# Two cross-attention stages rearranged: PSUM banks dealt out anew in the narrow one, VectorE's order and the query copies in the late one

## The chip, the cores and the metric

The kernel runs on one core of a Trainium2 chip. A core has five engines that run side by side and meet only at semaphores: TensorE (PE in the profile; PEld is its weight load), VectorE (DVE), ScalarE (ACT), GpSimd (POOL) and SyncE (SP), which issues the DMAs here. Matrix products land in PSUM, which has eight banks of 2 KiB in each of its 128 partitions; the other tensors lie in SBUF. The metric is device time in microseconds for one execution.

## The reference, cut to what matters

A two-layer decoder works on `x` of 128 sequences of 64 tokens with 128 channels, and every sub-layer is a residual on a layer norm. Six blocks follow each other: a wide self-attention, a cross-attention with narrow heads, a feed-forward block, two narrow self-attentions, and a wide cross-attention with a last tanh product. The change touches the second and the last.

```python
# narrow cross-attention: 16 heads of 8 channels, 64 keys, a mask
q = (layernorm(x) @ Wq.T + bq); k = (ctx @ Wk.T + bk); v = (ctx @ Wv.T + bv)
attn = softmax(q @ k.T / sqrt(8) + mask)
x = x + (attn @ v) @ Wo.T + bo
...
# late cross-attention: 16 heads of 64 channels, and the last product behind it
q = layernorm(x) @ Wq + bq; k = ctx @ Wk + bk; v = ctx @ Wv + bv
x = x + (softmax(q @ k.T / sqrt(64)) @ v) @ Wo + bo
x = x + tanh(layernorm(x) @ W0 @ W1 @ W2 + bias)
```

## The kernel before

The 8192 tokens are cut into 64 tiles of 128 tokens (two sequences), and `x` stays in SBUF as `w_x`. Each block of the model is a stage, and a stage is a software pipeline written out by hand. For each engine `skewed` takes a list of pieces with a lag: in step u the engine runs, in the order of the list, each piece for tile u minus its lag. Every engine works through its list in order, so a piece that waits on a semaphore holds up all that stands behind it in the list. The first 12 steps and the last ones are written out; the steps between them, 52 in both stages, are a loop whose body has four steps.

In the **narrow cross-attention** (tensors `ca_...`, norm `can_...`) a tile goes through: `measure` (VectorE, mean and variance), `rsqrt` (GpSimd), `offset` (VectorE, minus mean times rstd), `apply` (ScalarE, the normalised tile), `turn` and `turned` (transpose, copy out), `project` (queries, keys, values into one bank), `queries_keys` and `values` (ScalarE copies them out), `blocks` (GpSimd spreads the keys), `scores` (PE), `softmax` (VectorE adds the mask and takes the maximum), `shift` (GpSimd subtracts it), `exponent` (ScalarE), `turn_probs` (eight transposes into the two banks `pp0` and `pp1`), `probsT` (two copies out), `attend` (PE: numerator and denominator), `normalise` (VectorE: a reciprocal and a product), `output` (PE), `residual` (VectorE). Four banks, `ca_ss`, hold the scores in their lower halves. Numerator and denominator lie in the upper half of the first of these banks:

```python
num, den = ss[:, 0, 256:384], ss[:, 0, 384:512]
...
after(pe, o_done, t, 4)                                        # scores waits for normalise
...
pe.wait_ge(biased, min(t + 4, NT) * 2 if isinstance(t, int) else (t + 4) * 2)   # attend waits for softmax
```

So `scores` waits until `normalise` has emptied that half, and `attend` waits until `softmax` has read the other half of the same bank.

In the **late cross-attention** (tensors `xa_...`, norms `xan_...` and `lan_...`) the scores of a tile come from eight chunks of queries, of which ScalarE copies all out of PSUM (L909). VectorE's list has 11 pieces, among them `keys` (L947, two copies with the bias), `sums` (L972 and L975: row sums and their inverse), which releases GpSimd's `normalise` (L1015, one product over 128x1024), and `apply_last` (L496 with `lan_xn`), for which PE's `turn_last` (L794) waits. Behind `turn_last` PE's list has `turn` (L786), and the next step begins with `scores` (L851).

Of the kernel before, what the change touches and what calls it, by code (L numbers as in the profile page):

```python
# [710 lines left out]
def wide_cross_attention(k):  # L711
# [6 lines left out]
    with ExitStack() as ctx:  # L718
# [32 lines left out]
        with nc.Block() as block:  # L751
# [27 lines left out]
            def _(pe):  # L779
# [102 lines left out]
            def _(act):  # L882
# [52 lines left out]
            def _(dve):  # L935
# [61 lines left out]
                def finish(t, four):  # L997
# [5 lines left out]
                skewed(dve, NT, [(3, turn_blocks), (5, residual), (7, finish), (2, softmax), (0, measure), (5, measure_last), (1, keys), (2, sums),  # L1003
                                 (0, apply), (5, apply_last), (4, copy_x)], 4)
# [18 lines left out]
def narrow_cross_attention(k):  # L1023
# [7 lines left out]
    with ExitStack() as ctx:  # L1031
# [16 lines left out]
        off = sb("off", [P, 2])  # L1048
# [13 lines left out]
        y_psum, xb_done, x_done, off_done = sem("y_psum"), sem("x_plus_bias"), sem("x"), sem("offset")  # L1062

        with nc.Block() as block:
# [18 lines left out]
            def _(pe):  # L1083
                def turn(t, four):
# [4 lines left out]
                    after(pe, x_done, t, 7)  # L1089
# [13 lines left out]
                def scores(t, four):  # L1103
# [4 lines left out]
                    after(pe, o_done, t, 4)  # L1108
# [7 lines left out]
                def attend(t, four):  # L1116
# [4 lines left out]
                    pe.wait_ge(biased, min(t + 4, NT) * 2 if isinstance(t, int) else (t + 4) * 2)  # L1121
# [13 lines left out]
                def turn_probs(t, four):  # L1135
                    after(pe, exp_done, t)
                    for b in range(2):
                        after(pe, p_done, t, 1, per=2)
# [776 lines left out]
```

## Time and profile before

| | us |
|---|---|
| median of 3 runs (2395.14 to 2398.44) | 2395.47 |
| the profiled execution, its own time | 2399.14 |
| span of that execution in the trace | 2397.3 |
| narrow cross-attention, first statistics to last residual | 545.4 to 904.9 |
| late cross-attention, first statistics to the end | 1690.6 to 2397.3 |

The profile follows one execution. Its own time is 1.8 us more than the span of its instructions and 3.7 us above the median. A row of the timeline gives the start of a group of like instructions, its length, engine, line, operation, names and count; a bracket at its end is idle time of the engine before it and what ended it.

### The profile page before, as it was taken

The page shows a single profiled execution, that of the slowest core. Times are in us where ns is not written, and L with a number is a line of the kernel's source. Part 1 is how long each engine was busy: PE and PEld are TensorE (multiplying, and loading weights), DVE is VectorE, ACT ScalarE, POOL GpSimd, SP SyncE. Part 2 cuts the span into 40 slices and gives each one's busy share as a digit, 9 for nine tenths or more (in the row PEclk, how much of TensorE's full clock was granted, in tenths as well). Part 3 has the DMA queues.
Part 4 walks back from the last instruction along what each step waited for, and adds up shares of the span by engine and source line. Part 5 has one row for each costly group of instructions (what it writes and reads, how often), then busy time and mean ns, then how long its engine had stood idle before and what let it go on. Part 6 is the DMA issues. An engine that isn't in the chain of part 4 may idle for free. (4 is left out here: it accounts for less than half of the span.)

```text
span 2397.3 us, 89507 instructions
## 1 busy us (share of the span) xinstructions
PE 2110.9 (88%) x32271; PEld 1771.4 (74%) x32271; DVE 1924.7 (80%) x5225; ACT 1668.8 (70%) x4485; POOL 1200.5 (50%) x1151
## 2 busy tenths in 40 slices
PE   7999999997777771537999979999799999999997
PEld 7888888885555550235888858888688888888886
DVE  3888888877999986996777667776498999999995
ACT  1676666666777775646888858888476776777674
POOL 0333333326777764107999869999132333333332
PEclk9999999998999995857999989999899999999998
DMA  5000000001111100001000000000133333333333
GB/s 125 3 0 0 0 0 0 0 1 32 31 30 30 30 25 1 1 0 37 1 0 0 0 2 1 0 0 0 52 110 105 115 117 111 115 109 118 113 112 91
DMA packets 112239, 96.98 MB, mean 40 GB/s; under 512 B 24259, under 2 KB 103430, under 8 KB 112134
## 3 DMA queue, kind: packets, MB, share of 16 engines
q1 hardware_dynamic: 108722, 94.39, 12.8%
q10 hardware_dynamic: 3412, 1.19, 0.2%
q8 instruction: 66, 1.08, 0.2%
q14 instruction: 39, 0.32, 0.0%
HBM read 53.59 MB, written 41.94 MB: 40 GB/s over the span
## 5 line engine op out<-in xcount | busy, mean ns | idle before, releaser
L706 POOL TENSOR_TENSOR sa_sc<-sa_sc,sa_rs 128x1024 f32<-128x1024 f32 x64 | 121.8, 1904 | 311.1 <-DVE sa_rs L682 311.1
L1870 POOL TENSOR_TENSOR lo_qk_r<-lo_qk_ms,w_neg_half 128x20 f32<-128x20 f32 x64 | 226.9, 3546 | 22.3 <-DVE lo_qk_ms L1792 22.3
L1870 POOL TENSOR_TENSOR gl_qk_r<-gl_qk_ms,w_neg_half 128x20 f32<-128x20 f32 x64 | 226.3, 3536 | 14.3 <-DVE gl_qk_ms L1792 14.0
L486 POOL TENSOR_TENSOR xan_ve<-xan_mv,w_eps_ln 128x1 f32<-128x1 f32 x64 | 12.1, 189 | 352.8 <-DVE xan_mv L480 352.8
L917 ACT ACTIVATE xa_vx<-xa_oo 64x512 f32<-64x512 f32 x256 | 151.3, 591 | 43.1 <-PE xa_oo L817 38.3
L1015 POOL TENSOR_TENSOR xa_sc<-xa_sc,xa_rs 128x1024 f32<-128x1024 f32 x64 | 122.2, 1909 | 107.3 <-DVE xa_rs L975 107.3
L930 ACT ACTIVATE xa_oT<-xa_oo 128x512 f32<-128x512 f32 x128 | 69.5, 595 | 131.4 <-PE xa_oo L864 131.4
L651 ACT ACTIVATE sa_oT<-sa_oo 128x512 f32<-128x512 f32 x128 | 69.5, 595 | 117.6 <-PE sa_oo L594 117.6
L827 PEld LDWEIGHTS xa_qs<-xan_xT,late_x_wq 128*128 128x128 f32 x1024 | 124.4, 192 | 30.6 <-issue 30.6
L909 ACT ACTIVATE xa_qT<-xa_qs,late_x_bq 128x128 f32<-128x128 f32 x512 | 138.9, 383 | 1.6
L558 PE MATMUL sa_qs<-san_xT,w_a_wq 128*128 128x128 f32 x1024 | 134.0, 285 | 5.4 <-DVE sa_sc L668 5.0
L838 PE MATMUL xa_pp<-xa_cT,late_x_wk 128*128 128x128 f32 x1024 | 131.2, 283 | 0.2 <-DMA xa_cT<-ctxT_kept 0.2
L875 PE MATMUL xa_yy<-late_x_wo,xa_oT 128*128 128x128 f32 x1024 | 128.6, 280 | 1.8 <-ACT xa_oT L930 1.8
L558 PEld LDWEIGHTS sa_qs<-san_xT,w_a_wq 128*128 128x128 f32 x1024 | 121.9, 195 | 10.1 <-DVE sa_sc L668 7.4
L1617 PE MATMUL lo_ss<-lo_qT,lo_kz 128*128 128x256 f32 x512 | 127.9, 393 | 1.4 <-ACT lo_kz L1678 0.9
L1617 PE MATMUL gl_ss<-gl_qT,gl_kz 128*128 128x256 f32 x512 | 127.7, 393 | 1.4 <-ACT gl_kz L1678 0.9
L603 PE MATMUL sa_yy<-w_a_wo,sa_oT 128*128 128x128 f32 x1024 | 126.6, 277 | 1.2 <-ACT sa_oT L651 1.2
L1256 POOL TENSOR_TENSOR ca_sc<-ca_sc,ca_mx 128x1024 f32<-128x1024 f32 x64 | 121.7, 1902 | 11.1 <-DVE ca_mx L1226 8.2
L838 PEld LDWEIGHTS xa_pp<-xa_cT,late_x_wk 128*128 128x128 f32 x1024 | 125.1, 200 | 0.8 <-DMA xa_cT<-ctxT_kept 0.5
L827 PE MATMUL xa_qs<-xan_xT,late_x_wq 128*128 128x128 f32 x1024 | 124.6, 275 | 0.0
L875 PEld LDWEIGHTS xa_yy<-late_x_wo,xa_oT 128*128 128x128 f32 x1024 | 122.7, 196 | 2.5 <-ACT xa_oT L930 2.5
L603 PEld LDWEIGHTS sa_yy<-w_a_wo,sa_oT 128*128 128x128 f32 x1024 | 121.0, 194 | 1.7 <-ACT sa_oT L651 1.7
(323 smaller groups left out, 6714.0 us busy)
## 6 DMA issues: line engine op xcount, KB each, us to landing
blocks<-xa_tb SPq DMA_DIRECT2D x64, 512.0 KB, 2.7
xa_pt<-blocks SPq DMA_DIRECT2D x256, 128.0 KB, 2.9
w_x<-in_x_dram SPq DMA_DIRECT2D x8, 512.0 KB, 7.5
ca_cx<-in_ctx_dram SPq DMA_DIRECT2D x64, 64.0 KB, 1.8
ctxT_kept<-ca_xcT SPq DMA_DIRECT2D x64, 64.0 KB, 1.6
xa_cT<-ctxT_kept SPq DMA_DIRECT2D x64, 64.0 KB, 1.8
out_dram<-xa_out SPq DMA_DIRECT2D x64, 64.0 KB, 1.6
ca_mask<-in_mask_BxSxS_ff_dram SPq DMA_DIRECT2D x64, 32.0 KB, 1.7
```

The source lines that it names most:

```text
L558: last = pe.matmul(qs[b][:, c * P:(c + 1) * P], k["a_wq"][:, ch * P:(ch + 1) * P], norm["xT"][:, s, :], start=True, stop=True)
L603: last = pe.matmul(yy[:, 0:D], oT[:, s, n % 2, n // 2, :], k["a_wo"][:, n, :], start=(n == 0), stop=(n == 7))
L706: pool.tensor_tensor(v, v, bcast(rs[:, s, :], 2, S), ALU.mult).then_inc(prob_done, 1)
L827: final = pe.matmul(qs[b][:, c * P:(c + 1) * P], k["x_wq"][:, ch * P:(ch + 1) * P], norm["xT"][:, s, :], start=True, stop=True)
L838: final = pe.matmul(pp[b][:, c * P:(c + 1) * P], k["x_wk"][:, ch * P:(ch + 1) * P], cT[:, s, :], start=True, stop=True)
L875: final = pe.matmul(yy[:, 0:D], oT[:, s, n % 2, n // 2, :], k["x_wo"][:, n, :], start=(n == 0), stop=(n == 7))
L909: act.activation(qT[:, s, ch, :], qs[b][:, c * P:(c + 1) * P], ACT.Identity, bias=k["x_bq"][:, ch:ch + 1]).then_inc(q_done, 1)
L917: act.activation(vx[u * 64:u * 64 + 64, four, b, :, :, :].rearrange("p m e d -> p (m e d)"), oo[u][b * 64:b * 64 + 64, :], ACT.Copy).then_ ...
L1015: pool.tensor_tensor(v, v, bcast(rs[:, s, :], 2, S), ALU.mult).then_inc(prob_done, 1)
L1256: pool.tensor_tensor(sc[:, four, :, :], sc[:, four, :, :], bcast(mx[:, s, :], 2, S), ALU.subtract).then_inc(shifted, 1)
L1617: last = pe.matmul(ss[b][:, g * 256:(g + 1) * 256], kz[:, s, b, 2 * g:2 * g + 2, :].rearrange("p g j -> p (g j)"), qT[:, s, b, :, :].rearr ...
L1870: pool.tensor_tensor(qk_r[:, s, :], qk_ms[:, s, :], k["neg_half"][:, 0:NQK], ALU.pow).then_inc(sg["qk_r"], 1)
```

## The change: what it does

In the narrow cross-attention the two PSUM banks of the turned probabilities become one (`pp`), and numerator and denominator get the freed bank (`nd`). `turn_probs` and `probsT` are split into two rounds of four transposes and one copy each; the second round on PE waits until the copy of the first is done. The waits of `scores` on `normalise` and of `attend` on `softmax` go. `offset` moves from VectorE to GpSimd, as two products on one column. The lists of PE, ScalarE and VectorE are put in another order, and `output` and `residual` come one step earlier. In the late cross-attention chunks 4 to 7 of the queries are copied out by VectorE in one instruction, with a semaphore of its own for which `scores` waits too, and VectorE's list is put in another order.

```diff
@@ wide_cross_attention
                 def scores(t, four):
-                    after(pe, q_done, t, per=8)
+                    after(pe, q_done, t, per=4)
+                    after(pe, q2_done, t)
...
-                    for b in range(2):
-                        act.wait_ge(q_psum, t * 2 + b + 1)
-                        for c in range(4):
-                            ch = 4 * b + c
-                            act.activation(qT[:, s, ch, :], qs[b][:, c * P:(c + 1) * P], ACT.Identity,
-                                           bias=k["x_bq"][:, ch:ch + 1]).then_inc(q_done, 1)
+                    act.wait_ge(q_psum, t * 2 + 1)
+                    for c in range(4):
+                        act.activation(qT[:, s, c, :], qs[0][:, c * P:(c + 1) * P], ACT.Identity,
+                                       bias=k["x_bq"][:, c:c + 1]).then_inc(q_done, 1)
...
+                def queries(t, four):
+                    s = four % 2
+                    after(dve, s_psum, t, 2)
+                    after(dve, q_psum, t, per=2)
+                    dve.tensor_tensor(qT[:, s, 4:8, :], qs[1][:, :].rearrange("p (c i) -> p c i", c=4),
+                                      bcast(k["x_bq"][:, 4:8], 2, P), ALU.add).then_inc(q2_done, 1)
...
-                skewed(dve, NT, [(3, turn_blocks), (5, residual), (7, finish), (2, softmax), (0, measure), (5, measure_last), (1, keys), (2, sums),
-                                 (0, apply), (5, apply_last), (4, copy_x)], 4)
+                skewed(dve, NT, [(5, residual), (7, finish), (3, turn_blocks), (2, softmax), (0, measure), (5, measure_last), (2, sums),
+                                 (1, keys), (1, queries), (0, apply), (5, apply_last), (4, copy_x)], 4)
@@ narrow_cross_attention
-        pp = [ps("pp0"), ps("pp1")]
+        pp, nd = ps("pp"), ps("nd")
...
-        num, den = ss[:, 0, 256:384], ss[:, 0, 384:512]
+        num, den = nd[:, 0:P], nd[:, P:2 * P]
...
-                    after(pe, o_done, t, 4)
...
-                    pe.wait_ge(biased, min(t + 4, NT) * 2 if isinstance(t, int) else (t + 4) * 2)
...
+                        after(pe, exp_done, t)
+                        if b == 0:
+                            after(pe, p_done, t, 1, per=2)
+                        else:
+                            pe.wait_ge(p_done, t * 2 + 1)
...
-                skewed(pe, NT, [(3, scores), (2, project), (1, turn), (6, attend), (5, turn_probs), (7, output)], 4)
+                skewed(pe, NT, [(6, attend), (3, scores), (5, turn_probs(0)), (2, project), (1, turn), (5, turn_probs(1)), (6, output)], 4)
...
-                skewed(act, NT, [(2, queries_keys), (1, turned), (2, values), (4, exponent), (5, probsT), (0, apply)], 4)
+                skewed(act, NT, [(5, probsT(0)), (2, queries_keys), (1, turned), (5, probsT(1)), (2, values), (4, exponent), (0, apply)], 4)
...
-                skewed(dve, NT, [(8, residual), (0, measure), (3, softmax), (6, normalise), (0, offset)], 4)
+                skewed(dve, NT, [(7, residual), (0, measure), (6, normalise), (3, softmax)], 4)
...
+                    pool.tensor_tensor(neg_mean[:, s:s + 1], norm["mv"][:, s, 0:1], neg_one[:, :], ALU.mult).then_inc(nm_done, 1)
                     norm_rsqrt(k, norm, pool, t, s)
+                    after(pool, norm["rstd_done"], t)
+                    pool.tensor_tensor(off[:, s:s + 1], neg_mean[:, s:s + 1], norm["rstd"][:, s:s + 1], ALU.mult).then_inc(off_done, 1)
```

Two places show the new order. The first is one step of PE in the narrow cross-attention. Before, it is `scores` (L1113), `project`, `turn`, `attend` (L1127, L1131, into `ca_ss`), the eight transposes of the probabilities (L1141) and `output` (L1150):

```order
L1113 MATMUL ca_ss<-ca_kz,ca_qT 64x256 x8
L1099 MATMUL ca_m<-ca_xcT,w_c_wq 128x128
L1100 MATMUL ca_m<-ca_xcT,w_c_wk 128x128
L1101 MATMUL ca_m<-w_c_wv,ca_xcT 128x128
L1090 MATMUL ca_m<-w_constant,can_xn 128x128
L1091 MATMUL ca_m<-w_constant,ca_cx 128x128
L1127 MATMUL ca_ss<-ca_pt,ca_vz 32x64 x16
L1131 MATMUL ca_ss<-ca_pt,ca_vo 32x128 x8
L1141 MATMUL ca_pp<-w_constant,ca_sc 128x128 x8
L1150 MATMUL ca_m<-w_c_wo,ca_oT 128x128
```

After the change the same step on PE, with line numbers of the changed kernel (L1118 is `scores`, L1148 a round of `turn_probs`, L1131 and L1135 `attend`, L1157 `output`):

```order
L1131 MATMUL ca_nd<-ca_pt,ca_vz 32x64 x16
L1135 MATMUL ca_nd<-ca_pt,ca_vo 32x128 x8
L1118 MATMUL ca_ss<-ca_kz,ca_qT 64x256 x8
L1148 MATMUL ca_pp<-w_constant,ca_sc 128x128 x4
L1105 MATMUL ca_m<-ca_xcT,w_c_wq 128x128
L1106 MATMUL ca_m<-ca_xcT,w_c_wk 128x128
L1107 MATMUL ca_m<-w_c_wv,ca_xcT 128x128
L1096 MATMUL ca_m<-w_constant,can_xn 128x128
L1097 MATMUL ca_m<-w_constant,ca_cx 128x128
L1148 MATMUL ca_pp<-w_constant,ca_sc 128x128 x4
L1157 MATMUL ca_m<-w_c_wo,ca_oT 128x128
```

`attend` now opens the step, and the transposes stand in two groups with `project` and `turn` between them.

The second place is the later part of a step of VectorE in the late cross-attention. Before, from the statistics of the last norm on:

```order
L480 BN_AGGR lan_mv<-lan_stats 128x2
L947 TENSOR_TENSOR xa_kT<-xa_pp,late_x_bk 128x512 x2
L972 TENSOR_REDUCE xa_sm<-xa_sc 128x16
L975 RECIPROCAL xa_rs<-xa_sm 128x16
L496 TENSOR_SCALAR xan_xn<-w_x,xan_mv,xan_rstd 128x128
L496 TENSOR_SCALAR lan_xn<-w_x,lan_mv,lan_rstd 128x128
L987 TENSOR_TENSOR xa_xb<-w_x,w_x_row 128x128
L967 STREAM_TRANSPOSE xa_tb<-xa_sc 128x1024
L982 TENSOR_TENSOR w_x<-xa_yy,xa_xb 128x128
L1001 TENSOR_TENSOR xa_out<-xa_yy,w_x 128x128
L954 TENSOR_REDUCE xa_mx<-xa_qs 128x8 x2
```

After the change VectorE has there:

```order
L480 BN_AGGR lan_mv<-lan_stats 128x2
L978 TENSOR_REDUCE xa_sm<-xa_sc 128x16
L981 RECIPROCAL xa_rs<-xa_sm 128x16
L953 TENSOR_TENSOR xa_kT<-xa_pp,late_x_bk 128x512 x2
L945 TENSOR_TENSOR xa_qT<-xa_qs,late_x_bq 128x512
L496 TENSOR_SCALAR xan_xn<-w_x,xan_mv,xan_rstd 128x128
L496 TENSOR_SCALAR lan_xn<-w_x,lan_mv,lan_rstd 128x128
L993 TENSOR_TENSOR xa_xb<-w_x,w_x_row 128x128
L988 TENSOR_TENSOR w_x<-xa_yy,xa_xb 128x128
L1007 TENSOR_TENSOR xa_out<-xa_yy,w_x 128x128
L973 STREAM_TRANSPOSE xa_tb<-xa_sc 128x1024
L960 TENSOR_REDUCE xa_mx<-xa_qs 128x8 x2
```

The row sums and their inverse moved ahead of the key copies, the query copy stands between the keys and the two norms, and the block transpose (`xa_tb`) moved behind the residual and the output sum.

## Rows read from the trace of the kernel before

**Rows 1.** The page's chain that ended last: share of the span by line.

```profile
PE xa_pp L838 5%; PE xa_oo L817 4%; PE xa_yy L875 4%; PE xa_qs L827 4%; PE xa_qs L851 3%; PE xa_oo L864 2%; PE xa_misc L801 1%; PE xa_misc L786 1%; PE xa_misc L794 0%; ACT xa_vx L917 0%; ACT xa_qT L909 0%; DMA blocks<-xa_tb 0%; DMA xa_pt<-blocks 0%; PE xa_yy L808 0%; DVE lan_xn L496 0%
```

**Rows 2.** Windows, four tiles each: length; PE, PEld, DVE, ACT, POOL busy; clock; DMA.

```profile
690.42:712.15 21.73, 17.26 (x339) 12.76 (x328) 20.01 (x38) 17.17 (x45) 16.41 (x21) 1.00 0.11 30
2011.45:2053.03 41.58, 41.06 (x740) 35.32 (x741) 38.93 (x73) 29.52 (x72) 13.29 (x20) 1.00 0.35 114
```

**Rows 3.** Timeline, narrow stage, one step of VectorE and GpSimd: start, length in us.

```profile
700.35 0.29 DVE L1234 TENSOR_TENSOR ca_oT<-ca_ss,ca_rden 128x128 f32<-128x128 f32 x1
700.56 0.75 DVE L1212 SCALAR_TENSOR_TENSOR ca_off<-can_mv,can_rstd 128x1 f32<-128x1 f32 x1
701.24 0.28 DVE L1240 TENSOR_TENSOR w_x<-ca_m,ca_xb 128x128 f32 x1
...
696.85 0.19 POOL L486 TENSOR_TENSOR can_ve<-can_mv,w_eps_ln 128x1 f32<-128x1 f32 x1 [0.86 <-DVE can_mv L480]
...
699.40 1.90 POOL L1256 TENSOR_TENSOR ca_sc<-ca_sc,ca_mx 128x1024 f32<-128x1024 f32 x1
```

**Rows 4.** Timeline, narrow stage, the same step of ScalarE and PE.

```profile
697.42 0.37 ACT L1169 ACTIVATE ca_kT<-ca_m,w_c_bk 128x128 f32<-128x128 f32 x1
697.67 0.38 ACT L1171 ACTIVATE ca_qT<-ca_m,w_c_bq 128x128 f32<-128x128 f32 x1
698.06 0.38 ACT L1163 ACTIVATE ca_xcT<-ca_m 128x256 f32<-128x256 f32 x1
699.36 0.94 ACT L1177 ACTIVATE ca_vz<-ca_m 64x64 f32<-64x64 f32 x4 [0.92 <-PE ca_ss L1131]
700.33 1.06 ACT L1183 ACTIVATE ca_sc<-ca_sc 128x1024 f32<-128x1024 f32 x1
701.41 1.09 ACT L1190 ACTIVATE ca_pt<-ca_pp 128x512 f32<-128x512 f32 x2
...
696.18 0.49 PE L1099 MATMUL ca_m<-ca_xcT,w_c_wq 128*128 128x128 f32 x2
...
696.73 0.39 PE L1101 MATMUL ca_m<-w_c_wv,ca_xcT 128*128 128x128 f32 x2
...
699.24 1.09 PE L1141 MATMUL ca_pp<-w_constant,ca_sc 128*128 128x128 f32 x8
...
700.90 0.69 PE L1113 MATMUL ca_ss<-ca_kz,ca_qT 32*64 32x256 f32 x16 [0.35 <-DVE ca_oT L1234]
```

**Rows 5.** Timeline, late stage, end of a step: VectorE, ScalarE, GpSimd, then PE.

```profile
2006.01 1.29 DVE L947 TENSOR_TENSOR xa_kT<-xa_pp,late_x_bk 128x512 f32<-128x512 f32 x2
...
2008.63 0.26 DVE L496 TENSOR_SCALAR xan_xn<-w_x,xan_mv,xan_rstd 128x128 f32 x1
2008.81 1.97 DVE L496 TENSOR_SCALAR lan_xn<-w_x,lan_mv,lan_rstd 128x128 f32 x1
...
2008.92 2.17 ACT L909 ACTIVATE xa_qT<-xa_qs,late_x_bq 128x128 f32<-128x128 f32 x8
...
2008.80 1.90 POOL L1015 TENSOR_TENSOR xa_sc<-xa_sc,xa_rs 128x1024 f32<-128x1024 f32 x1 [1.71 <-DVE xa_rs L975]
...
2008.89 1.95 PE L875 MATMUL xa_yy<-late_x_wo,xa_oT 128*128 128x128 f32 x16
...
2010.83 0.33 PE L794 MATMUL xa_misc<-w_constant,lan_xn 128*128 128x128 f32 x1
2011.14 0.30 PE L786 MATMUL xa_misc<-w_constant,xan_xn 128*128 128x128 f32 x1
2011.45 1.16 PE L851 MATMUL xa_qs<-xa_kT,xa_qT 64*64 64x64 f32 x64
...
2022.17 0.34 PE L851 MATMUL xa_qs<-xa_kT,xa_qT 64*64 64x64 f32 x8 [0.45 <-issue]
```

**Rows 6.** Timeline, second narrow self-attention: a transpose, then scores, on PE.

```profile
1489.22 0.27 PE L1591 MATMUL lo_misc<-w_constant,lo_hn 128*128 128x128 f32 x1
1489.36 0.89 PE L1617 MATMUL lo_ss<-lo_qT,lo_kz 128*128 128x256 f32 x3
```

More of the change, by code:

```diff
@@ L1088, in turn @@
                     after(pe, xT_done, t, 1)
-                    after(pe, x_done, t, 7)
+                    after(pe, x_done, t, 6)
                     pe.transpose(m1[:, 0:P], norm["xn"][:, s, :], ident).then_inc(norm["xT_psum"], 1)
@@ L1133, in attend, with turn_probs, piece @@
                     last.then_inc(a_psum, 1)
[L1135 to L1138, printed above, removed]
+                def turn_probs(b):
+                    def piece(t, four):
+                        after(pe, exp_done, t)
[3 more added lines that the diff above has]
+                            pe.wait_ge(p_done, t * 2 + 1)
                         for n in range(4):
                             h = 8 * b + 2 * n
-                            last = pe.transpose(pp[b][:, n * P:(n + 1) * P],
-                                                sc[:, four, h:h + 2, :].rearrange("p a b -> p (a b)"), ident)
+                            last = pe.transpose(pp[:, n * P:(n + 1) * P], sc[:, four, h:h + 2, :].rearrange("p a b -> p (a b)"), ident)
                         last.then_inc(p_psum, 1)
+                    return piece
                 def output(t, four):
@@ L1183, in exponent, with probsT, piece @@
                     act.activation(sc[:, four, :, :], sc[:, four, :, :], ACT.Exp).then_inc(exp_done, 1)
-                def probsT(t, four):
-                    s = four % 2
-                    after(act, a_psum, t, 2)
-                    for b in range(2):
+                def probsT(b):
+                    def piece(t, four):
+                        s = four % 2
+                        after(act, a_psum, t, 2)
                         act.wait_ge(p_psum, t * 2 + b + 1)
-                        act.activation(pt[:, s, 4 * b:4 * b + 4, :].rearrange("p a b -> p (a b)"), pp[b][:, :], ACT.Copy).then_inc(p_done, 1)
+                        act.activation(pt[:, s, 4 * b:4 * b + 4, :].rearrange("p a b -> p (a b)"), pp[:, :], ACT.Copy).then_inc(p_done, 1)
+                    return piece
                 def apply(t, four):
@@ L1206, in measure @@
                     norm_measure(k, norm, dve, tile_of(X, t), t, four % 2)
-                def offset(t, four):
-                    s = four % 2
-                    after(dve, norm["rstd_done"], t)
-                    after(dve, norm["xn_done"], t, 2)
-                    dve.scalar_tensor_tensor(out=off[:, s:s + 1], in0=norm["mv"][:, s, 0:1], scalar=-1.0, in1=norm["rstd"][:, s:s + 1],
-                                             op0=ALU.mult, op1=ALU.mult).then_inc(off_done, 1)
                 def softmax(t, four):
@@ L1258, in rsqrt @@
                 def rsqrt(t, four):
-                    norm_rsqrt(k, norm, pool, t, four % 2)
+                    s = four % 2
+                    after(pool, norm["mv_done"], t)
+                    pool.tensor_tensor(neg_mean[:, s:s + 1], norm["mv"][:, s, 0:1], neg_one[:, :], ALU.mult).then_inc(nm_done, 1)
+                    norm_rsqrt(k, norm, pool, t, s)
+                    after(pool, norm["rstd_done"], t)
+                    pool.tensor_tensor(off[:, s:s + 1], neg_mean[:, s:s + 1], norm["rstd"][:, s:s + 1], ALU.mult).then_inc(off_done, 1)
                 def blocks(t, four):
```

10 lines of the change are left out of this document (6 added, 4 removed).

## The prediction

> **What bounds the kernel now.** I read first the page's chain of work that ended last. It ends in the late cross-attention, and nearly all its lines there are PE's [rows 1]: the reader is to see that PE sets the end of the last stage. The chain says nothing of the narrow stage, so second I read the windows, one turn of each loop, four tiles [rows 2]. In the narrow stage a tile takes 21.73 / 4 = 5.43 us, and no engine fills that: VectorE is busy 20.01 / 4 = 5.00, PE 4.32, ScalarE 4.29, GpSimd 4.10. In the late stage a tile takes 41.58 / 4 = 10.40, PE is busy 41.06 of 41.58 and VectorE 38.93. Third I read one step of each timeline, to see what the fullest engine does in its time.
>
> Narrow stage [rows 3]: `offset` (L1212) works on one column and yet lasts 0.75 us. It ends at 701.31, and GpSimd's `shift`, begun at 699.40, ends at 701.30. `offset` cannot finish while `shift` runs. The product before it, L1234, keeps to 0.29 in the middle of the same `shift`. VectorE's next instruction starts 701.24 - 700.56 = 0.68 after `offset` did. So the present step is a ring: VectorE's row maximum releases `shift`, `shift` holds `offset`, `offset` holds VectorE's next step.
>
> Late stage [rows 5]: the same hold. `lan_xn` takes 1.97, its twin `xan_xn` just before it 0.26. It ends at 2010.78, with GpSimd's `normalise` (2008.80 + 1.90 = 2010.70) and 1.71 too late. PE's `turn_last` (L794) waits for it and starts 0.05 later, at 2010.83. PE would hardly have been ready sooner, since L875 has just drained (2008.89 + 1.95). But behind that wait the next single transpose (L786) comes 0.31 later and `scores` (L851) another 0.31 later. Eight such transposes in a row take 1.09 [rows 4], so each needs (1.09 - 0.27) / 7, about 0.12, if the last takes 0.27 like the one in [rows 6]; and where PE does not stand at a wait, `scores` follows a transpose after 0.14 [rows 6]. I read the excess as PE's own preparation of the next pieces (several waits each), which it does early when nothing holds it and late when `lan_xn` does. Where the loop turns round it is worse: from L851 at 2011.45 to the next at 2022.17 are 10.72, while the other three steps share 41.58 - 10.72, 10.29 each: 0.43 more, marked as a wait for nothing [rows 5].
>
> **The change, narrow part.** Without `offset`, VectorE's step could be 5.43 - 0.68 = 4.75. GpSimd takes two more products on a column, 0.19 each like L486 [rows 3], and some 0.1 each to hand over: 4.10 + 0.6 = 4.7. PE and ScalarE keep their work, 4.3 each. The removed waits cost nothing any more: `scores` has its banks for itself as soon as the mask is added. What is late next is a ring that the two rounds make. The exponential of one step must end before PE's first round of transposes, and ScalarE begins its next step with the copy of that round. Its length, from [rows 4]:
> PE: four transposes, then `project`: the eight take 1.09, so `project` can start 0.45 after the first, and it lasts from 696.18 to 697.12, 0.94: 1.39. To ScalarE 0.05 (the shortest hand-over seen, [rows 5]). The first copy lies inside that time. Then ScalarE: keys 0.25 (697.42 to 697.67), queries 0.26 and `turned` 0.27 (0.38 each, less the 0.12 by which the key copy and its follower overlap), second copy 0.50 (two took 1.09, pipelined), values 0.97 (699.36 to 700.33), exponential 1.06. Back to PE 0.26, as `scores` starts 0.26 after L1234 ends (700.64 to 700.90) [rows 3, 4].
> Sum: 1.39 + 0.05 + 0.25 + 0.26 + 0.27 + 0.50 + 0.97 + 1.06 + 0.26 = 5.01. With the short hand-over of 0.05 at the end it is 4.80; with no overlap between ScalarE's three copies (0.38 - 0.26 and 0.38 - 0.27 more) and a hand-over 0.05 longer, 5.29. I take 5.0: it is longer than the sums of VectorE and GpSimd, so it sets the step. The second round's transposes wait for the first copy: round one 0.55, hand-over 0.05, copy 0.59, hand-over 0.26 is 1.45, about when PE has done `project` and `turn` anyway, so I put this wait at nothing; uncovered it could cost 0.1, which the upper end holds. Gain: 0.43 a tile. Some 60 of the 64 tiles run at the steady step: 26 us. Bounds: 4.80 gives 38, 5.29 gives 8.
>
> **The change, late part.** Copies of half the queries go from ScalarE (eight in 2.17, so 1.09 less) to VectorE in one instruction of the form of half L947, 1.29 / 2 = 0.65 [rows 5]. Sums and inverse now come before the keys, so `normalise` starts about 1.29 + 0.65 = 1.94 before the norms are due, and lasts 1.90 with 0.08 to hand over. `lan_xn` then waits some 0.05 instead of 1.71. VectorE's tile becomes 9.73 - 1.71 + 0.65 = 8.67 busy [rows 2, 5], well under 10.3. Its queries wait for PE's last query product, and the norms follow within 0.65 + 0.26 + 0.26 = 1.2, while PE still runs L875 for 1.8. So `lan_xn` comes about 0.6 before PE asks for it. The block transpose comes later by residual and output sum, 0.5, and by their wait for PE's last transpose; the `blocks` transfers behind it are needed a step later. I cost that at nothing.
> PE's work is unchanged. What it can gain is the preparation: 0.31 - 0.12 and 0.31 - 0.14 = 0.36 a step, so 10.29 - 0.36 = 9.93; with the loop's 0.43 kept that is a mean of 10.04, with it gone 9.93. I take 9.97: 0.43 under 10.40, times the 52 steps in the loop, 22 us. The wait added to `scores` (for VectorE's half) stands behind `turn`, where one more wait is at most a third of the 0.17 excess there, 0.06 a tile or 3 us if it shows; hidden it is nothing, and I take nothing. In the first steps, before the pipeline is full, the eight copies lie on the path; 1.09 less in three of them is 3 us. Lower end: nothing but these 3. Upper end: 0.47 x 52 + 3 = 27.
>
> A rule of the Trainium skill bears on the hold. Its page "SBUF — State Buffer", section "Who interferes with whom", says that VectorE and GpSimd share one port pair as an exclusive lock, which an instruction with at most one SBUF input outside the two-port modes does not need. By it the key and query copies, which read PSUM and one SBUF operand, run beside `normalise` and the whole 1.71 goes. The trace agrees as far as L1234 (0.29, one input from PSUM) stands against L1212 (0.75, both from SBUF) under one `shift` [rows 3].
>
> **Sum.** 26 + 22 + 3 = 51 us. On the profiled execution, 2399.1 (2397.3 and 1.8 around it), that is 2348; it stood 3.7 above the median of the runs, 2395.5, from which 51 less is **2344**.
>
> **The rivals.**
> *Only the narrow stage gains* (2 in 10). The 0.31s are what those waits cost PE in this loop, wherever it stands, and the local stage has fewer of them. Late part: the 3 us of the start alone. 2395.5 - 29 = 2366.
> *The ring of the two rounds takes nearly all back* (1 in 10). With 5.29 the narrow part is worth 8, the late 25: 2362. It speaks for it that ScalarE's `turned` may wait for `turn`, which now stands behind four transposes.
> *The hold stays, the slower side* (6 in 100). If the copies of keys and queries are held by `normalise` as `lan_xn` was, VectorE has its hold of 1.71 and 0.65 more work. Occupied for 10.29 less the short wait before its row maxima, say 10.1, it comes to 10.75, and as its residual now waits for PE's last transpose I add 0.3: 11.0 a tile, 0.65 x 52 = 34 us lost against 26 won. 2403. It decides from a hold of about 1.2 us on. L1234 speaks against it.
> *The change doesn't act* (4 in 100). The narrow step stays near 5.4, since three engines lie within 0.7 of it and wait for each other, and PE's preparation stays: within 0.2%, which is 5 us and about what a measurement of this kernel tells from no change.
>
> **How the numbers follow.** The forecast has 60 in 100; its own range, from the bounds of the two terms, is 2330 (38 + 27) to 2358. The first two rivals are added up to 2372 (the first with a narrow step of 5.1): 2328 to 2374 leaves out the slower side, the case of no action and some of the edges, under 2 in 10. Faster by over 0.2%: 0.60 + 0.20 + 0.10 = 0.90. Same 0.04, slower 0.06.
>
> **What would show it.** Narrow: a step near 5.0, no one-column instruction on VectorE, GpSimd near 4.7 a tile, and PE's first round standing at ScalarE's exponential. A step of 4.75 with VectorE full would say that the ring is shorter than I made it. Late: `lan_xn` at about 0.26 to 0.3; L786 and `scores` 0.12 to 0.15 behind their forerunners; a loop of four near 40. If `lan_xn` is short and the 0.31s remain, the first rival holds; if `lan_xn` remains near 2, the third. The prediction is most easily wrong in the late part, where 22 us hang on reading two gaps of 0.31 as preparation that a late norm exposes.

## The result, and the profile after

The changed kernel takes 2329.84 us (median of four, 2326.87 to 2330.55), the kernel before 2395.30 in the same comparison: ratio 0.9725, 95% interval 0.9708 to 0.9742, 65 us off. 2344 was forecast, with a range of 2328 to 2374. The profiled execution took 2330.41, its span is 2328.6, 68.7 under that of before. By stage, from the first row statistics to the last residual or the end of the span: the narrow cross-attention fell from 359.8 (545.4 to 905.2, the end of the last residual) to 327.0 us, the late one from 706.7 to 670.2; the rest grew by 0.6. Between row maxima, as the mean over ten turns of the loop (the 13th to the 53rd), a narrow step fell from 5.43 to 4.77 and a late one from 10.40 to 9.94.

The page of the changed kernel: busy time by engine, and the chain that ended last by line.

```profile
PE 2076.8 (89%) x32271; PEld 1753.6 (75%) x32271; DVE 1832.8 (79%) x5225; ACT 1599.1 (69%) x4229; POOL 1218.7 (52%) x1280
...
PE xa_pp L838 5%; PE xa_qs L827 5%; PE xa_yy L876 5%; PE xa_oo L817 5%; PE xa_qs L852 3%; PE xa_oo L865 2%; PE xa_misc L801 1%; PE xa_misc L786 0%; PE xa_yy L808 0%; PE xa_misc L794 0%; DMA blocks<-xa_tb 0%; DMA xa_pt<-blocks 0%; DVE xa_sm L978 0%; DVE xa_tb L973 0%; ACT xa_sc L922 0%
```

`lan_xn` has left the chain [rows 1]; what is left of the late stage is PE's own work. Windows of the changed kernel over four tiles of each stage, columns as in [rows 2]:

```profile
690.44:709.47 19.03, 16.57 (x328) 12.43 (x328) 17.19 (x33) 16.68 (x45) 17.50 (x29) 1.00 0.13 35
1966.94:2006.70 39.76, 39.47 (x743) 34.66 (x741) 35.35 (x76) 25.43 (x56) 13.29 (x20) 1.00 0.38 119
```

In the narrow stage VectorE lost 2.8 us of busy time in four tiles and GpSimd gained 1.1; all four engines now lie between 4.1 and 4.4 a tile, in a step of 4.76. In the late stage PE is busy for 39.47 of 39.76.

Timeline of the changed kernel, some narrow steps, VectorE, ScalarE, then PE [rows 3, 4]:

```profile
698.85 0.29 DVE L1241 TENSOR_TENSOR w_x<-ca_m,ca_xb 128x128 f32 x1 [0.21 <-POOL ca_xb L1275]
...
699.53 0.18 DVE L480 BATCH_NORM_AGGREGATE can_mv<-can_stats 128x2 f32<-128x6 f32 x1 [0.19 <-DVE can_stats L476]
...
684.63 1.06 ACT L1190 ACTIVATE ca_sc<-ca_sc 128x1024 f32<-128x1024 f32 x1
...
689.33 1.06 ACT L1190 ACTIVATE ca_sc<-ca_sc 128x1024 f32<-128x1024 f32 x1
...
691.81 0.37 ACT L1176 ACTIVATE ca_kT<-ca_m,w_c_bk 128x128 f32<-128x128 f32 x1
...
694.03 1.06 ACT L1190 ACTIVATE ca_sc<-ca_sc 128x1024 f32<-128x1024 f32 x1
...
698.96 1.06 ACT L1190 ACTIVATE ca_sc<-ca_sc 128x1024 f32<-128x1024 f32 x1
...
690.44 0.66 PE L1148 MATMUL ca_pp<-w_constant,ca_sc 128*128 128x128 f32 x4
...
695.29 0.66 PE L1148 MATMUL ca_pp<-w_constant,ca_sc 128*128 128x128 f32 x4
...
700.07 0.66 PE L1148 MATMUL ca_pp<-w_constant,ca_sc 128*128 128x128 f32 x4
```

A ring is a closed chain of work and waits; no step can be shorter than it. The ring of the forecast goes from PE's first round at 690.44 over the keys at 691.81 to the end of the exponential at 694.03 + 1.06 = 695.09, which is 4.65, and with a hand-over of 0.05 it is 4.70. It sets three steps of every four: all through the loop the exponentials start 4.70 apart, and PE's first round follows 0.05 after the exponential (690.39 to 690.44). The fourth step, where the loop turns round, takes 4.92 to 4.97, here from 694.03 to 698.96. In it `attend` starts 0.80 after `output` (692.85 to 693.65) where it otherwise starts 0.44 to 0.49 after (688.15 to 688.59), and the first round comes 0.20 after the exponential (695.09 to 695.29). VectorE does not set the step: it is busy for 4.30 of 4.76, and it waits for its own statistics in every step and for GpSimd's `copy_x` in every second one.

Timeline of the changed kernel, end of a late step, VectorE, GpSimd, then PE over a turn of the loop and one step further [rows 5]:

```profile
1963.79 1.22 DVE L953 TENSOR_TENSOR xa_kT<-xa_pp,late_x_bk 128x512 f32<-128x512 f32 x2
...
1965.99 0.34 DVE L496 TENSOR_SCALAR lan_xn<-w_x,lan_mv,lan_rstd 128x128 f32 x1
...
1963.96 1.90 POOL L1021 TENSOR_TENSOR xa_sc<-xa_sc,xa_rs 128x1024 f32<-128x1024 f32 x1 [0.49 <-DVE xa_rs L981]
...
1966.94 0.27 PE L786 MATMUL xa_misc<-w_constant,xan_xn 128*128 128x128 f32 x1
1967.50 1.16 PE L852 MATMUL xa_qs<-xa_kT,xa_qT 64*64 64x64 f32 x64 [0.29 <-issue]
...
1976.92 0.27 PE L808 MATMUL xa_yy<-w_constant,xa_th 128*128 128x128 f32 x1
1977.03 0.27 PE L794 MATMUL xa_misc<-w_constant,lan_xn 128*128 128x128 f32 x1
1977.14 0.27 PE L786 MATMUL xa_misc<-w_constant,xan_xn 128*128 128x128 f32 x1
1977.35 0.87 PE L852 MATMUL xa_qs<-xa_kT,xa_qT 64*64 64x64 f32 x44
```

`lan_xn` takes 0.34 and ends at 1966.33, half a microsecond before PE uses it (1966.83). L794, L786 and scores follow their forerunners after 0.11, 0.11 and 0.21. At the turn of the loop scores comes 0.56 after L786, so some 0.35 of the turn's excess is still there.

### The profile page after: what moved, and what is told of

Its sections match the earlier page's. It is cut to its first block and busy times, and to the rows that moved or that the text cites. A ratio compares the mean times of both kernels' runs of the same rounds, so it can differ in the third digit from the quotient of the medians.

```text
span 2328.6 us, 89415 instructions
## 1 busy us (share of the span) xinstructions
PE 2076.8 (89%) x32271; PEld 1753.6 (75%) x32271; DVE 1832.8 (79%) x5225; ACT 1599.1 (69%) x4229; POOL 1218.7 (52%) x1280
## 5 line engine op out<-in xcount | busy, mean ns | idle before, releaser
L827 PEld LDWEIGHTS xa_qs<-xan_xT,late_x_wq 128*128 128x128 f32 x1024 | 124.4, 192 | 30.6 <-issue 30.6
L827 PE MATMUL xa_qs<-xan_xT,late_x_wq 128*128 128x128 f32 x1024 | 124.6, 275 | 0.0
L817 PE MATMUL xa_oo<-late_x_wv,xa_cT 128*128 128x512 f32 x256 | 121.1, 595 | 0.0
```

Of the source, the lines that this page charges most:

```text
L817: pe.matmul(oo[u][:, :].rearrange("p (m c) -> p m c", m=4), cT[:, s, :], wv[:, :, u, :], start=True, stop=True).then_inc(v_psum, 1)
L827: final = pe.matmul(qs[b][:, c * P:(c + 1) * P], k["x_wq"][:, ch * P:(ch + 1) * P], norm["xT"][:, s, :], start=True, stop=True)
```

## The experiments

Twelve kernels, each against the kernel before on the same chip. Steps are means over ten turns of the loop between row maxima, as above.

| kernel | median us | ratio to before, 95% | narrow step | late step |
|---|---|---|---|---|
| before | 2395.3 | 1 | 5.43 | 10.40 |
| changed | 2329.8 | 0.9708 to 0.9742 | 4.77 | 9.94 |
| narrow_alone | 2357.4 | 0.9817 to 0.9856 | 4.79 | 10.40 |
| late_alone | 2365.8 | 0.9853 to 0.9895 | 5.44 | 9.95 |
| offset_moved_alone | 2391.0 | 0.9965 to 0.9984 | 5.34 | 10.43 |
| apply_before_copies | 2374.2 | 0.9888 to 0.9917 | 5.04 | 10.41 |
| lists_with_old_banks | 2492.7 | 1.0365 to 1.0426 | 7.68 | 9.95 |
| offset_back_on_vectore | 2328.9 | 0.9695 to 0.9729 | 4.77 | 9.95 |
| copy_in_the_ring | 2334.9 | 0.9726 to 0.9761 | 4.93 | 9.95 |
| copy_in_the_gap | 2326.9 | 0.9695 to 0.9732 | 4.77 | 9.94 |
| order_without_split | 2345.0 | 0.9769 to 0.9806 | 4.77 | 10.19 |
| split_without_order | 2592.5 | 1.0803 to 1.0843 | 4.77 | 14.50 |
| late_norm | 2361.3 | 0.9840 to 0.9876 | 4.79 | 10.52 |
| load_behind_norm | 2327.8 | 0.9702 to 0.9745 | 4.77 | 9.99 |

**The two halves.** `narrow_alone` is the kernel before with the change's hunks in `narrow_cross_attention`; `late_alone` has those in `wide_cross_attention`.

> The kernel before with the narrow stage of the change alone. Theory: the two parts touch different stages and the stages do not overlap by more than their ramps, so the narrow stage falls from 359.8 us to about 327, the late stage keeps its 707 and its loop of four its 41.6: about 33 us off, 2362. Rival, that the two parts help or hinder each other (the narrow stage runs beside something of the late one): the gain differs from 33 by more than 5 us.

> The kernel before with the late stage of the change alone. Theory: the narrow stage keeps its 359.8 us, the late one falls from 706.7 to about 670, of which the steady loop gives 23 to 24 and the first steps about 12: about 36 us off, 2359. Rival, that the gain in the first steps comes from the narrow stage's earlier end or other order: the late stage then stays above 677.

The steps fell just as in the changed kernel. In `narrow_alone` 39 us went, 6 more than forecast and so past the rival's bound of 5: the narrow stage took 324.6 us, and the late stage, untouched, was also 8.5 shorter (698.2). In `late_alone` the late stage took 670.6, as forecast, and 31 us went by the medians (37.6 by the profiled spans). By the medians the parts bring 70 us apart and 65 together, which intervals of 4 to 5 us to either side of each do not tell apart; by the profiled spans they bring 79 and 69. What both bring is in the late stage's first steps. From the first to the twelfth row maximum the late stage takes 121.4 us before, 113.5 in `narrow_alone`, 109.1 in `late_alone`, 109.0 with both.

**Is it the held `offset`?** In `offset_moved_alone` the kernel before gets the change's two products on GpSimd in place of VectorE's `offset`, and nothing else; of the edit, VectorE's list is shown.

```diff
-                skewed(dve, NT, [(8, residual), (0, measure), (3, softmax), (6, normalise), (0, offset)], 4)
+                skewed(dve, NT, [(8, residual), (0, measure), (3, softmax), (6, normalise)], 4)
```

> The kernel before with offset alone moved from VectorE to two products on GpSimd; banks and lists of the narrow stage stay. Theory A (the one-column instruction held under the shift is what the narrow step costs): VectorE's step loses 0.68, the step of 5.43 falls to 4.8 to 4.95, 27 to 35 us off. Theory B (the shared bank, with scores waiting for the output and attend for the mask, sets the step as much): the step stays at 5.3 to 5.4, at most 8 us off.

Theory B's number, though the bank is not yet the longest ring here: the step lost 0.1 of the 0.68. Timeline of `offset_moved_alone`, one step, VectorE, ScalarE, then PE:

```profile
700.25 0.96 DVE L1224 RECIPROCAL ca_rden<-ca_ss 128x128 f32<-128x128 f32 x1 [0.28 <-PE ca_ss L1131]
...
700.25 0.94 ACT L1177 ACTIVATE ca_vz<-ca_m 64x64 f32<-64x64 f32 x4 [0.59 <-PE ca_ss L1131]
...
702.30 1.08 ACT L1190 ACTIVATE ca_pt<-ca_pp 128x512 f32<-128x512 f32 x2
703.27 0.49 ACT L1196 ACTIVATE can_xn<-w_x,ca_off,can_rstd 128x128 f32 x1
...
704.10 0.32 PE L1090 MATMUL ca_m<-w_constant,can_xn 128*128 128x128 f32 x1 [0.86 <-ACT can_xn L1196]
```

In a window of four tiles VectorE is busy 17.73 of 21.29 us, so it no longer sets the step; now it waits for PE's `attend`. PE's list puts `attend` behind `turn`, and `turn` waits 0.86 for ScalarE's `apply`. ScalarE has `apply` behind values, exponential and copies, and values waits for the `attend` of the step. That closes a second ring: values starts at 700.25, when `attend` has ended, `turn` starts at 704.10, and then comes the next `attend`. As the step lost no more than 0.1, the ring must have been there before, at nearly the same length.

`apply_before_copies` cuts that ring in `offset_moved_alone` with one more edit.

```diff
-                skewed(act, NT, [(2, queries_keys), (1, turned), (2, values), (4, exponent), (5, probsT), (0, apply)], 4)
+                skewed(act, NT, [(2, queries_keys), (1, turned), (2, values), (4, exponent), (0, apply), (5, probsT)], 4)
```

> offset_moved_alone with one edit: in ScalarE's narrow list apply stands before the two copies of the probabilities, not behind them. Its trace shows a second ring beside VectorE's: attend ends, values 0.97, exponential 1.08, copies 0.97 to 1.05, apply 0.49 with its hand-over, turn 0.34, attend 1.15: 5.3 a step. Theory A (this ring is why the step stayed at 5.34 when offset left VectorE): without the copies in it the ring is 4.3, and VectorE with the shared bank (mask 1.29, hand-over, attend 1.15, reciprocal 0.96, product 0.32, residual, statistics) sets the step, at 5.0 to 5.25: 5 to 20 us faster than offset_moved_alone. Theory B (the shared bank's ring alone sets 5.34): the step stays within 0.04 of 5.34.

Theory A: 5.04, 16.9 us faster than `offset_moved_alone`. What holds now stands on PE, in the timeline of `apply_before_copies`:

```profile
701.32 0.65 PE L1127 MATMUL ca_ss<-ca_pt,ca_vz 128*32 128x64 f32 x32 [0.52 <-DVE ca_sc L1214]
...
704.00 0.69 PE L1113 MATMUL ca_ss<-ca_kz,ca_qT 32*64 32x256 f32 x16 [0.35 <-DVE ca_oT L1227]
```

Both waits belong to the bank that scores shares with numerator and denominator: `attend` waits for the mask to be added, scores for `normalise`.

**Order or bank?** `lists_with_old_banks` is the changed kernel with the old banks and their waits, and each pair of rounds in one piece:

```diff
-        num, den = nd[:, 0:P], nd[:, P:2 * P]
+        num, den = ss[:, 0, 256:384], ss[:, 0, 384:512]
...
+                    after(pe, o_done, t, 3)
...
+                    pe.wait_ge(biased, min(t + 3, NT) * 2 if isinstance(t, int) else (t + 3) * 2)
...
-                skewed(pe, NT, [(6, attend), (3, scores), (5, turn_probs(0)), (2, project), (1, turn), (5, turn_probs(1)), (6, output)], 4)
+                skewed(pe, NT, [(6, attend), (3, scores), (5, turn_probs), (2, project), (1, turn), (6, output)], 4)
...
-                skewed(act, NT, [(5, probsT(0)), (2, queries_keys), (1, turned), (5, probsT(1)), (2, values), (4, exponent), (0, apply)], 4)
+                skewed(act, NT, [(5, probsT), (2, queries_keys), (1, turned), (2, values), (4, exponent), (0, apply)], 4)
```

> The changed kernel with the narrow stage's banks of before: numerator and denominator back in the scores' first bank with the waits that this needs, the probabilities in two banks, turned and copied in one piece; the lists of the engines, offset and residual as changed. Theory A (the order of the lists is what shortens the step: PE's attend and ScalarE's values, exponential, copies and apply no longer follow one another in one ring): two rings remain, that of the shared bank (attend 1.15, reciprocal 0.96, product 0.32, scores 0.69, mask 1.29, hand-overs 0.3 to 0.6: 4.7 to 5.0) and that of ScalarE (hand-over 0.26, eight transposes, project 0.94, the three copies 0.78, values 0.97, exponential 1.06: 5.0): a step of 4.8 to 5.05. Theory B (the shared bank is the cost): the step stays at 5.3 or above.

Neither: 7.68, far over both. Timeline of `lists_with_old_banks`, one step in the order of the waits:

```profile
699.55 0.69 PE L1119 MATMUL ca_ss<-ca_kz,ca_qT 32*64 32x256 f32 x16 [1.59 <-DVE ca_oT L1233]
...
700.86 1.08 ACT L1196 ACTIVATE ca_pt<-ca_pp 128x512 f32<-128x512 f32 x2 [2.76 <-PE ca_pp L1147]
...
702.50 1.04 POOL L1269 TENSOR_TENSOR ca_kz<-ca_kT,w_constant 128x512 f32<-128x512 f32 x1 [2.54 <-ACT ca_kT L1175]
...
704.17 0.29 DVE L1239 TENSOR_TENSOR w_x<-ca_m,ca_xb 128x128 f32 x1 [1.29 <-POOL ca_xb L1273]
```

Scores waits for `normalise`; behind it in PE's list stand the transposes and `project`; the copies and keys wait for those, GpSimd's `kz` and `copy_x` for the keys, VectorE's residual for `copy_x`, and `normalise` stands behind the residual. I had summed two rings and missed this third, through all four engines. PE's clock adds to it: of the four steps from 732.41 on, three take 6.97 to 7.81 at a granted clock of 0.94 to 1.00 and one takes 8.87 at 0.50. The one at 1.00 (2.4 GHz) takes the 6.97, still far over both theories. The new order is good only with the free bank. The free bank with the old lists was not run: with one bank for the probabilities the second round would have to wait in the old lists too, so it would not be the bank alone.

`offset_back_on_vectore` puts `offset` at the end of VectorE's changed list and takes the two products from GpSimd.

```diff
-                skewed(dve, NT, [(7, residual), (0, measure), (6, normalise), (3, softmax)], 4)
+                skewed(dve, NT, [(7, residual), (0, measure), (6, normalise), (3, softmax), (0, offset)], 4)
```

> The changed kernel with offset back at the end of VectorE's list; banks, rounds and the other lists as changed. Theory A (the hold costs 0.7 wherever offset stands under a shift, and VectorE is at 4.3 without it): if it is held again, the step is 5.0 to 5.4, 15 to 40 us lost. Theory B (right behind the row maximum it gets in before the shift has begun, or VectorE's slack of 0.4 to 0.5 takes most of it): the step is 4.76 to 4.9, at most 8 us lost. The length of the instruction tells which: 0.2 or 0.75.

Theory B: 4.77, nothing lost. Timeline of `offset_back_on_vectore`:

```profile
687.63 0.15 DVE L1220 SCALAR_TENSOR_TENSOR ca_off<-can_mv,can_rstd 128x1 f32<-128x1 f32 x1
...
687.79 1.90 POOL L1264 TENSOR_TENSOR ca_sc<-ca_sc,ca_mx 128x1024 f32<-128x1024 f32 x1
```

Right behind the row maximum it starts 0.16 before `shift`, takes 0.15, not 0.75 [rows 3], and is done when `shift` starts. The move to GpSimd has no part in the gain of the changed kernel.

**Does the ring of the two rounds set the step?** The same unused ScalarE copy is put once into the ring and once behind `apply`.

```diff
-                skewed(act, NT, [(5, probsT(0)), (2, queries_keys), (1, turned), (5, probsT(1)), (2, values), (4, exponent), (0, apply)], 4)
+                skewed(act, NT, [(5, probsT(0)), (2, queries_keys), (1, turned), (5, probsT(1)), (5, extra), (2, values), (4, exponent), (0, apply)], 4)
```

> The changed kernel with one more ScalarE copy, 128x128 (0.25 pipelined, 0.38 alone), between the second copy of the probabilities and values; its result is not used. Theory A (the ring from PE's first round through ScalarE's list back to the next first round sets the step of 4.77): all of it is added, a step of 5.0 to 5.15, 15 to 24 us lost. Theory B (VectorE, PE or GpSimd with their hand-overs set it): the step stays under 4.85.

> The changed kernel with the same ScalarE copy at the end of ScalarE's list, behind apply, where ScalarE waits for PE's first round; its result is not used. Theory A (the ring passes through exponential, PE, first copy, and this copy lies beside PE's part): apply 0.49 and the copy 0.25 end 0.74 after the exponential, the first copy can start 0.26 + 0.55 + 0.05 = 0.86 after it: a step of 4.76 to 4.85, within 5 us of the changed kernel. Theory B (ScalarE's sum of work sets it): as in copy_in_the_ring, 5.0 or more.

Timeline of `copy_in_the_ring`, ScalarE, then PE:

```profile
689.03 1.06 ACT L1191 ACTIVATE ca_sc<-ca_sc 128x1024 f32<-128x1024 f32 x1
...
693.93 1.06 ACT L1191 ACTIVATE ca_sc<-ca_sc 128x1024 f32<-128x1024 f32 x1
...
698.91 1.06 ACT L1191 ACTIVATE ca_sc<-ca_sc 128x1024 f32<-128x1024 f32 x1
...
690.15 0.66 PE L1149 MATMUL ca_pp<-w_constant,ca_sc 128*128 128x128 f32 x4 [0.34 <-ACT ca_sc L1191]
```

In the ring the copy took 0.20 (start to start). Three steps of four grew by all of it, from 4.70 to 4.90; the one where the loop turns, which had a wait to spare, grew from 4.92 to 4.97 only to 4.98. That is the 0.15 a step, and 7 us of the narrow stage (334.4 against 327.0); by the medians it is 5 us, which the intervals do not tell apart. In the gap the copy cost nothing, and the pattern of 4.70 and 4.92 to 4.97 stayed. So ScalarE's sum does not count and its place does, and the ring of the two rounds sets the step except at the loop's turn. That is Theory A's mechanism, though its 5.0 to 5.15 was too high, as it took all steps to pay; B's 4.85 was too low.

**Late stage: order or split?** `order_without_split` is the changed kernel with all eight query copies on ScalarE; `split_without_order` has VectorE's late list in the old order, with the half copy behind the keys.

```diff
+                skewed(dve, NT, [(3, turn_blocks), (5, residual), (7, finish), (2, softmax), (0, measure), (5, measure_last), (1, keys), (1, queries), (2, sums),
+                                 (0, apply), (5, apply_last), (4, copy_x)], 4)
```

> The changed kernel with the late stage's eight query copies back on ScalarE; VectorE's new order stays. Theory A (the order is what frees lan_xn, the split of the copies is a help): the norms now have only the keys, 1.22, ahead of them under a normalise of 1.98 with its hand-over, so they are held for 0.5 to 0.7, but end before PE asks; loop of four 39.8 to 40.6, at most 11 us lost. Theory B (the split is needed, since scores waits for the eighth copy or the norms are still late): loop of four about 41.5, 20 us or more lost.

> The changed kernel with VectorE's late list in the order of before, the half query copy behind the keys. Theory A (the order frees lan_xn): the hold of lan_xn stays at 1 us or more, VectorE has 0.6 more to do, a loop of four of 42 to 44, 28 to 53 us lost against the changed kernel. Theory B (taking 1.09 from ScalarE is what gains): 40 to 40.5, at most 10 us lost.

The order alone gives 10.19, nearly half of the gain, and stays 15 us behind the changed kernel: between the two theories, since both parts count. Timeline of `order_without_split`, VectorE, GpSimd, ScalarE, PE:

```profile
1937.58 1.00 DVE L496 TENSOR_SCALAR xan_xn<-w_x,xan_mv,xan_rstd 128x128 f32 x1
1938.50 0.34 DVE L496 TENSOR_SCALAR lan_xn<-w_x,lan_mv,lan_rstd 128x128 f32 x1
...
1936.59 1.90 POOL L1015 TENSOR_TENSOR xa_sc<-xa_sc,xa_rs 128x1024 f32<-128x1024 f32 x1 [0.49 <-DVE xa_rs L975]
...
1937.90 2.18 ACT L909 ACTIVATE xa_qT<-xa_qs,late_x_bq 128x128 f32<-128x128 f32 x8
...
1939.88 0.27 PE L786 MATMUL xa_misc<-w_constant,xan_xn 128*128 128x128 f32 x1
1940.37 1.16 PE L851 MATMUL xa_qs<-xa_kT,xa_qT 64*64 64x64 f32 x64 [0.21 <-issue]
```

Now `xan_xn` is held (1.00, until `normalise` ends at 1938.49), yet `lan_xn` ends a microsecond before PE asks, and L786 follows L794 after 0.11. Scores comes 0.43 to 0.49 behind L786, since the eighth copy ends only at 1940.08. That is what the split removes.

The split without the order makes the kernel 195 us slower than before, 263 slower than the changed one. Timeline of `split_without_order`, one late step on VectorE, then PE:

```profile
1999.69 0.69 DVE L945 TENSOR_TENSOR xa_qT<-xa_qs,late_x_bq 128x512 f32<-128x512 f32 x1 [2.30 <-PE xa_qs L827]
...
2001.88 1.97 DVE L496 TENSOR_SCALAR lan_xn<-w_x,lan_mv,lan_rstd 128x128 f32 x1
...
2003.91 0.48 PE L794 MATMUL xa_misc<-w_constant,lan_xn 128*128 128x128 f32 x1 [2.36 <-DVE lan_xn L496]
2004.21 0.45 PE L786 MATMUL xa_misc<-w_constant,xan_xn 128*128 128x128 f32 x1
2004.63 1.99 PE L852 MATMUL xa_qs<-xa_kT,xa_qT 64*64 64x64 f32 x64
```

VectorE stands 2.30 at PE's queries with sums and norms behind it; `lan_xn` is held as before, and PE waits 2.36 for it. Theory A had the hold and not this wait: it gave 42 to 44 for a loop of four that took 58. PE's clock adds to it here too: after the wait a transpose takes 0.45 to 0.48 where it took 0.27, scores 1.99 where it took 1.16, and the granted clock over four tiles is 0.85, a mean between the levels of 1.2 (0.5) and 2.4 GHz (1.0).

**Is it lateness of `lan_xn` that PE pays for?** One unused VectorE reduction (0.68) is put ahead of `lan_xn` in `late_norm`, behind it in `load_behind_norm`:

```diff
-                                 (1, keys), (1, queries), (0, apply), (5, apply_last), (4, copy_x)], 4)
+                                 (1, keys), (1, queries), (0, apply), (5, extra), (5, apply_last), (4, copy_x)], 4)
```

> The changed kernel with one more VectorE instruction (a maximum over 128x512, near 0.6 us, its result not used) between xan_xn and lan_xn in the late stage. Theory A (PE gains because lan_xn is ready before PE asks for it, so that PE prepares its next pieces early): lan_xn comes within 0.1 of PE's asking or later, the gaps of 0.3 around L794, L786 and scores and the loop's 0.43 come back at least in part, 0.2 to 0.4 a step, 10 to 20 us lost. Theory B (VectorE's idle 0.7 a step takes it and PE does not mind): under 4 us lost, gaps of 0.11 and 0.20 as they are.

> The same VectorE instruction as in late_norm, but behind lan_xn, ahead of the copy of x. Theory A (it is the lateness of lan_xn that counts, not VectorE's sum): under 4 us lost, PE's gaps as in the changed kernel. Theory B (VectorE's sum counts): the same loss as late_norm within 3 us.

Behind the norm it costs nothing that can be measured, ahead of it 31 us. Timeline of `late_norm`:

```profile
1941.93 0.34 DVE L496 TENSOR_SCALAR lan_xn<-w_x,lan_mv,lan_rstd 128x128 f32 x1
...
1942.06 0.27 PE L809 MATMUL xa_yy<-w_constant,xa_th 128*128 128x128 f32 x1
1942.33 0.33 PE L795 MATMUL xa_misc<-w_constant,lan_xn 128*128 128x128 f32 x1
1942.62 0.30 PE L787 MATMUL xa_misc<-w_constant,xan_xn 128*128 128x128 f32 x1
1943.08 1.16 PE L853 MATMUL xa_qs<-xa_kT,xa_qT 64*64 64x64 f32 x64 [0.15 <-issue]
```

`lan_xn` ends at 1942.27; PE could have used it at 1942.06 + 0.11 = 1942.17. The wait itself is 0.16 (0.27 from L809 on, less 0.11). But the next two starts are 0.29 and 0.46 behind, not 0.11 and 0.21, though `xan_xn` and the queries were there before `lan_xn`: 0.16 + 0.18 + 0.25 = 0.59, the 0.57 by which the step grew. Theory A was right on what counts, and its price, 0.2 to 0.4, was too low. What PE does in the two longer gaps the trace does not show; that it prepares the next pieces there is my reading.

## Why the prediction was right, point by point

The total came out by three terms that were all too small: 26 us for the narrow step was 33, 22 for the late step 23.5, and 3 for the start 12.4. That is 69 us by the profiled spans; by the medians 65 us went where 51 were forecast, and 2329.84 lies at the fast end of the range (2328), at the edge of the forecast's own (2330). The slow end of that own range, 2358, does not follow from the bounds of the two terms: both lower ends together, 8 and 3, give 2384.

**Narrow stage, the reading of the kernel before failed.** The step "the present step is a ring: VectorE's row maximum releases `shift`, `shift` holds `offset`, `offset` holds VectorE's next step", with 5.43 - 0.68 = 4.75 to follow, was wrong as a price: without `offset` the step is 5.34. The hold is there, but two more rings lay right under it, through ScalarE's list (5.34) and through the shared bank (5.04). The change breaks both by opening PE's step with `attend` and giving it a bank. "The removed waits cost nothing any more" passed over the waits that still held the step at 5.04 when the other two rings were cut.

**Narrow stage, the size.** The ring of the two rounds sets the step, as the forecast said, but I mis-sized it: 5.01 on paper, 4.70 in the trace, mostly because the hand-over from the exponential is 0.05 and not 0.26. With the longer step at the loop's turn the mean is 4.77. That this is also near the 4.75 which the forecast gave VectorE alone is chance, for VectorE is not full: the sign "a step of 4.75 with VectorE full" holds in the step and not in VectorE. So the gain was 0.66 a tile instead of 0.43, but over some 50 steps instead of 60, since from the first row maximum to the 13th it took 61.6 us before and 61.8 after: 33 us, not 26.

**Late stage, right.** `lan_xn` is free and half a microsecond early, and the gaps close: L794 to L786 from 0.30 to 0.11, L786 to scores from 0.33 to 0.20 (to 0.14 in my sum), and three more by 0.04 to 0.05 each that I had not counted (L808 to L794, scores to the `xa_oo` products behind them, and those to L801; the last two are as long as before in `order_without_split`, so they come with the split). The turn of the loop kept its 0.35 to 0.4. Together 0.45 a step where I took 0.43; times 52 that is 23.5 us, against 22. `late_norm` shows by itself that a late `lan_xn` opens the gaps. What I costed at nothing, the later block transpose and the wait for VectorE's half of the queries, shows as no wait of PE; whether the 0.06 by which scores stays above 0.14 is that added wait, no run tells.

**The port rule.** The Trainium skill, page "SBUF — State Buffer", section "Who interferes with whom", lets VectorE instructions with at most one SBUF input, outside the two-port modes, run beside GpSimd's, and says that of two that collide the first issued has its way. The traces agree on the first: the keys, from PSUM and one SBUF operand, take 1.22 in the changed kernel beside `normalise`, while `xan_xn`, with its operands in SBUF, was held for 1.00 in `order_without_split`; in which mode it ran no trace shows. Of the second they show one side: `offset`, begun under `shift`, was held for 0.75, and begun 0.16 ahead of it took 0.15, but there it was done when `shift` began, so no run here shows GpSimd held.

**The start, mis-sized.** 3 us forecast; from the first to the twelfth late row maximum it was 12.4. The split's share is seen in the first steps: from L827 to scores PE took 4.12 before, with 2.06 of waiting for the eight copies, and 3.32 after. But `narrow_alone` gains 7.9 of the 12.4 with the late stage of before, and 3.3 of that is one gap. Timeline of the kernel before, and then of `narrow_alone`, at the same pair of instructions, where PE goes from the twelve steps that are written out into the loop:

```profile
1807.95 0.30 PE L786 MATMUL xa_misc<-w_constant,xan_xn 128*128 128x128 f32 x1
1812.24 1.99 PE L851 MATMUL xa_qs<-xa_kT,xa_qT 64*64 64x64 f32 x64 [3.99 <-issue]
```

```profile
1771.52 0.30 PE L786 MATMUL xa_misc<-w_constant,xan_xn 128*128 128x128 f32 x1
1772.50 1.16 PE L851 MATMUL xa_qs<-xa_kT,xa_qT 64*64 64x64 f32 x64 [0.68 <-issue]
```

From L786 to scores there: 4.29 before, 4.03 and 3.77 in `offset_moved_alone` and `apply_before_copies`, 1.57 in `late_alone`, 0.98 in `narrow_alone`, 0.99 in the changed kernel. The traces show what goes with it. Among their DMA packets is one of 16 KB of the kind `instruction` (queue q8) near this place in all fourteen kernels. In the three with the long gaps it starts after L786 (1809.39 against 1807.95 in the kernel before), and scores starts 1.93 to 1.94 after it has landed (1810.31 to 1812.24). In the other eleven it has landed before L786 starts (at 1770.28 against 1771.52 in `narrow_alone`), and the gap is 0.88 to 1.61. So PE most likely waits there for a block of its own instructions; whose the packet is the trace does not say, and why it comes late in three kernels no run tests. After the long gap the granted clock is 0.50 for 6.8 us in the kernel before (1810.5 to 1817.3), and scores takes 1.99 there instead of 1.16.

**The rivals.** "Only the narrow stage gains" fell with the gaps at 0.11 and 0.20, "the ring takes nearly all back" with a ring of 4.70, and "the hold stays" with `lan_xn` at 0.34. The last has its place all the same: `split_without_order` keeps the hold and adds VectorE's work, and was slower by far more than the 11.0 a tile I gave it, as PE then waits too. No kernel of the twelve is faster than the changed one by more than the intervals; `copy_in_the_gap`, `offset_back_on_vectore` and `load_behind_norm` are level with it.

## What to carry to other kernels

A held instruction on the fullest engine is worth its hold only if no other ring is nearly as long: before pricing its removal, walk the rings through the other engines' lists, in list order, with every wait for a shared bank. An in-order engine that is the bound should never be the one that waits: its operands want to be early, since a wait of 0.16 us cost 0.57 a step here. Orders, banks and splits belong together: without its banks (`lists_with_old_banks`) or without VectorE's new order (`split_without_order`) the rest of this change is 97 and 195 us slower than the kernel before.

## What was not expected of the hardware

The 0.3 gaps are not a property of those instructions: the same pairs on PE follow after 0.11 and 0.20 when the input is there, after 0.30 and 0.45 when the input of the instruction ahead was 0.16 late. The turn of the late loop costs PE 0.35 to 0.4 of its own before and after the change, and the turn of the narrow loop 0.36. And the first entry into the late loop can cost PE 4 us or 1 us, in kernels whose late stage is the same, with an instruction transfer that lands late or early.
